# Routed experts on one core: 128-row blocks two groups forward, table-row loads after the transposes

## The reference, cut to what matters

```python
x = x + attention(layernorm(x), Wq, Wk, Wv)
xn = layernorm(x)
shared = (silu(xn @ shared_gate.T) * (xn @ shared_up.T)) @ shared_down.T
probs = sigmoid(xn @ router_w.T + routing_bias)
scores, indices = top_k(probs, 2)          # 2 of 8 experts for each of 4096 tokens
w[t, indices[t]] = scores[t] / sum(scores[t])
g = silu(xn @ gate_w[e]); u = xn @ up_w[e]  # 256 -> 512, e = 0..7
out = x + shared + sum_e w[:, e] * ((g * u) @ down_w[e])
```

## Time and profile before

| | us |
|---|---|
| median of 3 runs (lowest, highest) | 573.29 (572.55, 575.23) |
| the profiled execution | 578.4 |
| its span | 576.6 |
| PE busy | 521.9 (91%) |
| DVE busy | 371.8 (64%) |
| ACT busy | 306.5 (53%) |
| POOL busy | 290.2 (50%) |
| first matmul of the routed part, start | 277.08 |
| last matmul of the program, end | 561.47 |
| last add issued, start | 569.38 |

### The profile page before, as it was taken

How to read it: one execution, slowest core, us unless ns; L and a number is a source line. 1 busy time by engine, 2 the same in 40 slices (tenths; PEclk the granted TensorE clock), 3 DMA queues, 4 the chain that set the end, 5 groups by cost and what they waited for, 6 DMA issues and landing times. The chain is left out here.

```text
span 576.6 us, 14723 instructions
## 1 busy us (share of the span) xinstructions
PE 521.9 (91%) x4521; PEld 422.9 (73%) x4522; DVE 371.8 (64%) x933; ACT 306.5 (53%) x578; POOL 290.2 (50%) x236
## 2 busy tenths in 40 slices
PE   2797999798999999889799999999999999999970
PEld 1455788586777878778578888888888888888860
DVE  5579999879897978969645555455545455545440
ACT  4989778577768667544234443443444443444430
POOL 3654778557585846756014434533433343533443
PEclk9699999899999999989999999999999999999996
DMA  7988866929493948552455646565565555566523
GB/s 260 221 202 149 155 171 132 257 78 217 140 198 125 199 134 170 175 156 76 91 115 88 99 76 94 75 93 74 74 96 81 78 77 75 83 90 77 73 30 36
DMA packets 147551, 70.53 MB, mean 122 GB/s; under 512 B 122384, under 2 KB 140560, under 8 KB 147504
## 3 DMA queue, kind: packets, MB, share of 16 engines
q1 hardware_dynamic: 133904, 50.69, 42.1%
q0 software_dynamic: 13600, 19.22, 19.0%
HBM read 19.48 MB, written 23.54 MB: 75 GB/s over the span
## 5 line engine op out<-in xcount | busy, mean ns | idle before, releaser
L1767 PE MATMUL bank<-xn2t,w 128*128 128x256 f16 x1728 | 197.1, 273 | 2.9 <-DMA xn2t<-rows 2.5
L1767 PEld LDWEIGHTS bank<-xn2t,w 128*128 (+1 forms) x1728 | 168.5, 98 | 26.5 <-issue 2.8
L712 POOL DMA_INDIRECT out<-p,wm x56 | 89.2, 1593 | 115.2 <-DMA out<-p,wm 44.6
L1336 DVE SCALAR_TENSOR_TENSOR th<-th,bank 128x512 f32<-128x512 f32 x88 | 60.1, 683 | 75.3 <-ACT th L806 75.2
L1781 PE MATMUL bank<-w,h 128*128 (+1 forms) x840 | 98.5, 273 | 2.1 <-DVE z L1268 2.0
L1781 PEld LDWEIGHTS bank<-w,h 128*128 128x128 f16 x840 | 81.5, 98 | 13.5 <-DVE z L1268 3.5
L762 ACT ACTIVATE h<-th 128x512 f16<-128x512 f32 x72 | 45.2, 628 | 85.3 <-DVE th L1345 83.5
L806 ACT ACTIVATE th<-bank 128x512 f32<-128x512 f32 x88 | 52.5, 596 | 58.4 <-PE bank L1767 58.2
L1171 DVE TENSOR_TENSOR h<-th,h 128x512 f16<-128x512 f32 x72 | 49.8, 691 | 41.1 <-ACT h L762 41.1
L601 POOL TENSOR_TENSOR w<-wst,w 128x768 f16<-128x768 f32 x36 | 59.1, 1642 | 31.4 <-ACT w L762 31.1
L625 POOL DMA_INDIRECT rows<-xrow,sidx x56 | 57.4, 1026 | 27.5 <-DVE sidx L1328 15.9
(11 more groups left out here) (159 smaller groups left out, 728.3 us busy)
## 6 DMA issues: line engine op xcount, KB each, us to landing
wst<-w_all SPq DMA_DIRECT2D x36, 384.0 KB, 3.6
x<-x SPq DMA_DIRECT2D x8, 512.0 KB, 5.6
out<-x SPq DMA_DIRECT2D x8, 512.0 KB, 4.6
rows<-xrow POOLq DMA_DIRECT2D x1, 1192.5 KB, 7.3
rows<-xrow,sidx POOLq DMA_INDIRECT x56, 4.3
out<-p,wm POOLq DMA_INDIRECT x56, 4.0
wm<-rows SPq DMA_DIRECT2D x28, 9.0 KB, 1.8
xn2t<-rows SPq DMA_TRANSPOSE x28, 3.6
```

The source lines that it names most:

```text
L712: cc.indirect_dma_start(out, bass.IndirectOffsetOnAxis(ap=index, axis=0), part, None, compute_op=ALU.add).then_inc(y_out, 16)
L1336: d.scalar_tensor_tensor(out=tb, in0=tb, scalar=1.0, in1=G[half][:, :], op0=ALU.add, op1=ALU.mult).then_inc(f_sg, 1)
L1767: ins = mm(dst, w_ap(j, ws, m * MAT + k * I + (2 * half + i) * P, P), moving(ms * KD + k), start=(cnt == 0), stop=(cnt == 3 * KD - 1))
```

## The change

Three things are changed, all in the routed part.

1. **The singles run two groups forward.** In group i PE now takes the down product of single i+2 and the gate and up products of single i+3. The first two groups take five gate and up products of singles and four down products, the last group and the one before it take no gate and up product of a single, and the last group no single at all. Each engine follows: order of copies on ACT, of h on DVE, of adds on POOL (p2i-1, s(i+2), p2i), of loads on SP. The last two groups of adds are p23, s14, p24 and then p25, p26, p27.
2. **In SP's queue the transpose of a block stands ahead of its index load,** and the wait on `y_out` moves with the index load.
3. **At the entry** the two table reads of the pairs are made before the wait for the scattered rows, all four row transposes (p0, s0, s1, p1) are issued first, and the four index loads behind them.

```diff
+            def load_pair_rows(row, ring, read):
                 slot = ring % 2
-                row = sp.value_load(start_tab[0:1, ds(n, 1)], min_val=0, max_val=ROWS - TT)
-                gate(sp, ax_in[ring], seen, sp_past)
-                free_aux(used)
-                sp.dma_start(aux[...], rows[ds(row, TT), D:RC]...).then_inc(ax_in[ring], 16)
                 free_rows(read)
                 sp.dma_start_transpose(xt[...], rows[ds(row, TT), 0:D]...).then_inc(xt_in[slot], 16)
+            def load_pair_aux(row, ring, seen, used):
+                gate(sp, ax_in[ring], seen, sp_past)
+                free_aux(used)
+                sp.dma_start(aux[...], rows[ds(row, TT), D:RC]...).then_inc(ax_in[ring], 16)
...
             def first_group():                      # SP
                 hs_transpose(0, 0)
                 row = single_row(2)
                 load_single_rows(row, 0, 1)
                 hs_transpose(1, 1)
                 load_pair(2, 2, 2 * SHARED + 2, 0, 0)
+                load_single_aux(row, 0, 16, 48)
                 hs_transpose(2, 0)
-                load_single_aux(row, 0, 16, 16)
-                load_single(3, 1, 2, 16, 32)
-                load_pair(3, 3, 2 * SHARED + 4, 0, 16)
+                row = single_row(3)
+                load_single_rows(row, 1, 2)
+                load_pair(3, 3, 2 * SHARED + 4, 0, 0)
+                load_single_aux(row, 1, 16, 64)
...
-            def group(i, par, last=False):          # SP
-                load_pair(2 * i + 2, 2 - 2 * par, 4 * i + (2 * SHARED + 2), 8 * i + 8 * par, GROUP_ADDS * i - 16)
-                hs_transpose(i + 2, par)
-                if not last:
-                    load_single(i + 3, 1 - par, i + 2, 8 * i + (16 + 8 * par), GROUP_ADDS * i + 32)
-                load_pair(2 * i + 3, 3 - 2 * par, 4 * i + (2 * SHARED + 4), 8 * i + 8 * par, GROUP_ADDS * i + 16)
+            def group(i, par, single=True):
+                if not isinstance(i, int) or i > 2:
+                    hs_transpose(i + 2, par)
+                if single:
+                    row = single_row(i + 4)
+                    load_single_rows(row, par, i + 3)
+                load_pair(2 * i + 2, 2 - 2 * par, 4 * i + (2 * SHARED + 2), 8 * i + 8 * par, GROUP_ADDS * i)
+                if single:
+                    load_single_aux(row, par, 8 * i + (32 - 8 * par), GROUP_ADDS * i + 48)
+                load_pair(2 * i + 3, 3 - 2 * par, 4 * i + (2 * SHARED + 4), 8 * i + 8 * par, GROUP_ADDS * i + 32)
...
+            def first_groups():                     # POOL
+                y_add(0, 0, 16, 0)
+                y_add_single(0, 0, 16, 32)
+                y_add_single(1, 1, 16, 48)
+                y_add(1, 1, 16, 64)
...
             def first_groups():                     # PE
...
                 pe.wait_ge(xt_in[1], 16)
                 gate_up(t + 1, 0, j1, pair_moving(1), False)
+                down(t, j0)
                 single_down(0, 0)
-                down(t, j0)
                 single_gate_up(2, 0, 32)
+                gate_up(t + 1, 1, j1, pair_moving(1), False)
                 single_down(1, 1)
-                gate_up(t + 1, 1, j1, pair_moving(1), False)
+                j2 = expert(2)
+                pe.wait_ge(xt_in[0], 32)
+                gate_up(t + 2, 0, j2, pair_moving(0), False)
+                down(t + 1, j1)
+                single_gate_up(3, 1, 32)
+                gate_up(t + 2, 1, j2, pair_moving(0), False)
+                single_down(2, 0)
...
```

More of the change, by code:

```diff
@@ L439, in free_aux, with pair_row, single_row @@
                 gate(sp, y_out, used, sp_past)
-            def load_pair(n, ring, read, seen, used):
-                slot = ring % 2
-                row = sp.value_load(start_tab[0:1, ds(n, 1)], min_val=0, max_val=ROWS - TT)
+            def pair_row(n):
+                return sp.value_load(start_tab[0:1, ds(n, 1)], min_val=0, max_val=ROWS - TT)
+            def single_row(k):
+                return sp.value_load(start_tab[0:1, ds(k + PAIRS, 1)], min_val=0, max_val=ROWS - P)
+            def load_pair_rows(row, ring, read):
+                slot = ring % 2
+                free_rows(read)
+                sp.dma_start_transpose(
+                    xt[:, slot * 4 * TT:(slot + 1) * 4 * TT].rearrange("p (c r) -> p c r", r=TT),
+                    rows[ds(row, TT), 0:D].bitcast(F16)).then_inc(xt_in[slot], 16)
+            def load_pair_aux(row, ring, seen, used):
                 gate(sp, ax_in[ring], seen, sp_past)
@@ L449, in load_pair @@
                              ).then_inc(ax_in[ring], 16)
[L450 to L456, removed]
+            def load_pair(n, ring, read, seen, used):
+                row = pair_row(n)
+                load_pair_rows(row, ring, read)
+                load_pair_aux(row, ring, seen, used)
             def load_single_rows(row, slot, read):
@@ L470, in load_single_aux @@
                              rows[ds(row, P), D:RC]).then_inc(as_in[slot], 16)
[L472 to L476, removed]
             def hs_transpose(k, slot):
@@ L517, in _ @@
             first_group()
-            group(1, 1)
-            with sp.Fori(2, GROUPS - 2, 2) as i:
+            second_group()
+            group(2, 0)
+            group(3, 1)
+            with sp.Fori(4, GROUPS - 4, 2) as i:
                 for s in range(2):
                     group(i + s, s)
-            group(GROUPS - 2, 0, last=True)
+            group(GROUPS - 4, 0)
+            group(GROUPS - 3, 1, single=False)
+            group(GROUPS - 2, 0, single=False)
             sp.wait_ge(y_out, 32 * PAIRS + 16 * SINGLES)
@@ L1155, in _ @@
                     group(i + s, s)
-            group(GROUPS - 2, 0)
-            group(GROUPS - 1, 1, last=True)
+            group(GROUPS - 2, 0, single=False)
+            group(GROUPS - 1, 1, single=False, copy_single=False)
             last_copy()
@@ L1712, in ffn, with group @@
                 ffn_low(t, half)
-            def group(i, last=False):
+            def group(i, single=True):
                 t = 2 * i + SHARED
@@ L1717, in group @@
                     ffn(t, half)
-                if not last:
-                    single_h(i + 2)
+                if single:
+                    single_h(i + 3)
                 for half in range(2):
@@ L1730, in _ @@
             ffn(SHARED + 1, 1)
-            with dve.Fori(1, GROUPS - 1) as i:
+            ffn(SHARED + 2, 0)
+            single_h(3)
+            ffn(SHARED + 2, 1)
+            ffn(SHARED + 3, 0)
+            single_h(4)
+            ffn(SHARED + 3, 1)
+            with dve.Fori(2, GROUPS - 2) as i:
                 group(i)
-            group(GROUPS - 1, last=True)
+            group(GROUPS - 2, single=False)
+            group(GROUPS - 1, single=False)
         @block.tensor
@@ L2076, in first_group, with group @@
                 gate_up(t + 1, 0, j1, pair_moving(1), False)
+                down(t, j0)
                 single_down(0, 0)
-                down(t, j0)
                 single_gate_up(2, 0, 32)
+                gate_up(t + 1, 1, j1, pair_moving(1), False)
                 single_down(1, 1)
-                gate_up(t + 1, 1, j1, pair_moving(1), False)
-            def group(i, par, last=False):
+                j2 = expert(2)
[5 more added lines that the diff above has]
+                single_down(2, 0)
+                j3 = expert(3)
+                pe.wait_ge(xt_in[1], 32)
+                gate_up(t + 3, 0, j3, pair_moving(1), False)
+                down(t + 2, j2)
+                single_gate_up(4, 0, 48)
+                gate_up(t + 3, 1, j3, pair_moving(1), False)
+                single_down(3, 1)
+            def group(i, par, single=True, down_single=True):
                 t = 2 * i + SHARED
@@ L2127, in _ @@
                     group(i + s, s)
-            group(GROUPS - 2, 0)
-            group(GROUPS - 1, 1, last=True)
+            group(GROUPS - 2, 0, single=False)
+            group(GROUPS - 1, 1, single=False, down_single=False)
             last_down()
```

107 lines of the change are left out of this document (69 added, 38 removed).

## The result

The changed kernel takes 584.25 us (median of 5 runs, 583.14 to 587.90) against 573.29 for the kernel before (median of 5, 571.86 to 577.74): ratio 1.0168, 95% interval 1.0129 to 1.0207, slower (the two medians alone give 1.0191). A later comparison of the same two on another occasion gave 1.0221 (1.0171 to 1.0271). The forecast was 580.0 in a range of 575 to 585, so the direction and most of the path were right, and one term was far too small. The measured median lies at the upper end of the range; the forecast alone spanned 576 to 582.

The account below looks back on a forecast made before the run. PE's matmuls were taken to bound the routed part, so only PE's idle time and the tail could change. + 7.6 (s3's rows) + 2.5 (clock) + 0.6 (h transposes) - 4.0 (tail) = + 6.7 on 573.29: 580.0 us, range 575 to 585.

Parts of the forecast that it names:

- s3's rows: Entry: s3's row transpose queues behind s2's index load, which waits for adds; PE idles 8.3 us, + 7.6 us, bounds 6.5 to 8.7.
- the reason given for the start of p0's copies: Entry: ACT is held until 292.09 by the landing of s0's h, so p0's copies can't start much before 296.50.
- The clock: s3's block after the long idle gap: PE falls to half clock, + 2.5 us, bounds 0 to 2.5.
- The middle: Middle groups: h transposes issued later, slack 0.8 us with the median landing; + 0.6 us in all, least 0, most 5.
- The rival with the late h transposes: Middle: PE waits for ten h transposes by 0.5 us each, 4.4 more than taken, 584.4 us; chance 0.13.
- named for a right forecast: Gap about 8 us, block at clock 0.50, third add about 305, last matmul about 572, last pair's add about 2 us later.
- the signs named for a wrong one: No gap over 3 us from 300 to 320, many small gaps before singles' downs, or last add over 4 us behind PE.
- The tail: End: last pair's first add 2.1 instead of 6.05 us behind PE's last matmul, - 4.0 us, bounds 3.7 and 4.2.
- The sum: Whole kernel: + 7.6 + 2.5 + 0.6 - 4.0 = + 6.7 us, giving 580.0 us.
- The first case: Entry: PE never waits for s3, entry 0.8 ahead and tail gives 4.0: 568.5 us; chance 0.10.
- the even one: Entry: wait for s3 half as long (4 us) and clock stays up, 573.1 us; chance 0.08.
- the last (the tail gives nothing): Tail: chain of adds falls behind again, p27's add stays 6 us behind PE's last matmul, 584.0 us; chance 0.07.

Follow-up runs that it names:

- second profile: Kernel before and changed kernel each run once more, unchanged: before 574.4 us (one run), changed kernel ratio 1.0221 to before.
- e1: Changed kernel with s3's row transpose moved ahead of s2's index load in SP's queue: 582.0 us, ratio 1.0109 to the kernel before.
- e5: Changed kernel with 28 filler matmuls keeping PE busy while it waits for s3's rows: one run, 312.5 us from S to the end of the span.
- e2: Changed kernel with, in the middle, each single's h transpose moved ahead of the index load that waits for an add: 582.9 us, ratio 1.0106.
- e8: Changed kernel with old entry, row and h transposes first, and each single's index load moved to the next group: 576.8 us, ratio 0.9990.
- e9: Changed kernel, its new entry kept, with row and h transposes first and each single's index load moved to the next group: 573.6 us, ratio 0.9941.
- e3: Changed kernel with s3's rows ahead of s2's index load and, in the middle, h transposes ahead of waiting index loads: 576.5 us, ratio 0.9990.
- e4: Kernel before with only the new order of table reads, transposes and index loads at the entry: 575.9 us, ratio 0.9994.

## Why the prediction was right, and where it was not

**s3's rows: + 7.6 forecast, + 7.9 measured** (44.0 - 36.1; 6.3 in the second profile). The add of s0 was forecast 33.2 us after S (305.0 - 271.79) and came 33.3 after it (302.06 - 268.74). Each link is in the chain shown above, and e1 takes the gap away by putting s2's index load behind the two transposes. That the size fits so well is partly luck. The first profile has the slow blocks at s0, 1.7 us, which push p0's down and with it the whole chain back; in the second, without them, the add of s0 came 32.0 us after S (303.45 - 271.47), and the term is 6.3, just under the lower bound of 6.5. PE's gap was 7.0 us in both, where 8.3 was forecast. And the reason given for the start of p0's copies didn't hold: ACT didn't wait for s0's h in the changed kernel, it copied p0's result from 293.74, 1.3 us after PE had gone on from p0's down (292.47). This down lay so late after S that the copy still came where the forecast had it (25.0 us after S against 24.7).

**The clock: + 2.5 forecast, + 1.9 measured** (4.52 - 2.59), 1.4 in the second profile of the changed kernel, and 2.9 in e2, where the block takes 5.09 us and the one behind it is slow as well. The earlier trace rows was the right row, and e5 shows the cause.

The rule of the Trainium skill (TensorE: Matmul & The Clock Gate, HAM oscillation) holds here as far as it says that a long idle gap brings half clock; the block ran at a granted clock of 0.55.

**The middle: + 0.6 forecast, + 7.3 measured** (262.8 - 1.9 - 253.6). This is the step that failed, by size. The mechanism was the one named, h transposes behind the index load that waits for an add and behind the rows of the next pair, but I priced it with the median landing of before and a slack of 0.8 us. Three things were missing. The slack is that of a chain that runs on time, and in the groups behind the entry it doesn't: s5's h was 2.4 us late and took the clock down again (its next block took 3.87 us for 2.59). Behind such a down the next block comes some 0.6 us late each time, even where the down itself hardly waits, which I put down to the table read between them (argued, as said at e2); in the kernel before this shows at 0.3 us at most. And the landing was slower than the median of before. From issue to landing the transposes of the h of s5 to s14 took 3.1 to 4.2 us in both profiles of before; in the changed kernel they took 5.1, 5.1, 5.4, 3.8, 5.1, 3.7, 3.8, 3.6, 4.3 and 5.0, which uses up most or all of those 4.3 to 5.6 us. The singles whose down or the block behind it came 0.6 us late or more are s5, s6, s7 and s9, four of the five with a landing of 5.0 us or more. No run shows why they are slower. In e2, where h is issued some 12 us ahead, landings of up to 5.8 us cost nothing.

In the first profile the waits at the downs, the reads behind them and the slow block at s5 add up to 6.9 of the 7.3 us, and e2 gives 5.7 back (260.9 to 255.2). The 1.6 us that are left are hardly more than the 1.3 by which the two profiles of before differ. The rival with the late h transposes had this price, 0.5 us for each of ten, and its number, 584.4 us, is nearly the one that was measured (584.25), though the loss isn't spread over ten but sits at four or five of them. It had a chance of 0.13, and that the measured time lies within the range is owed to the room left for it, not to the forecast's own sum. The signs agree: the gap, the slow block, the third add and the short tail came as named for a right forecast, but PE's last matmul ended at 575.5 instead of about 572 although S was 3 us earlier, and one of the signs named for a wrong one, gaps at the singles' downs ended by a DMA into `v`, is there in part (two of them in the first profile).

**The tail: - 4.0 forecast, - 4.5 measured** in the first profiles (6.05 to 1.5), and - 0.9 in the second ones (3.5 to 2.7). All ten profiles in which the singles are forward have p27's add at E + 0.8 to E + 2.7, the three in which they aren't at E + 3.3 to E + 6.1. So the mechanism is right, and its price is nearer to 2 to 3 us than to 4: I had taken a single execution for typical. The steps of the chain came as forecast (p24's to p27's adds at E - 17.9, - 11.2, - 4.8 and + 1.5, against - 18.2, - 11.2, - 4.2 and + 2.1). The 3.3 us that I took for the least from the end of a down to its add isn't a floor in the tail, where p27's add comes 0.8 to 2.7 us behind it; held to it, my own sum would have given E + 3.3.

**The sum** was + 6.7; from S the profiles say 317.4 - 304.8 = + 12.6, and the medians + 11.0. The forecast has the direction and the order of size; the missing 6 us lie in the middle. The first case (faster, PE never waits) and the even one fell with the 7 us gap, and the last (the tail gives nothing) with p27's add at E + 1.5.

Left open: why e8 and e9 differ by 0.5% in their runs, how much of the 2.3 to 3.6 us gained from S in e8 is real, and why the h transposes take longer to land in their new place.

## What to carry to other kernels

In a queue that runs in order a load whose wait depends on the far end of the pipeline must stand behind everything that is needed sooner, however small it is; when work is moved forward, look up every wait of its queue again, with what must now have happened before it. A hidden latency of half a microsecond (here, as argued, a table read) comes out as soon as the wait in front of it is late. And take a price from the place where the change will run: slack that a settled pipeline has in the middle is not there in its first groups, and the landing time of a transfer in its old place (3.1 to 4.2 us here) is not that in its new one (up to 5.4).

## What the runs showed that I had not expected

- The part of the program that no kernel here changes started its last product between 266.6 and 271.8 us (S), and this spread of 5 us is as large as most effects studied. Two profiles can't be compared end to end.
- The clock can fall after shorter gaps too. In the second profile of before, with 0.81 us of idleness, a block of 2.8 us and then 2.30 us of idleness, p0's 24 matmuls took 4.30 us from start to start instead of 2.62, while in the first profile they took their usual time after gaps of 0.85 and 2.50:

```profile
269.06 2.79 PE L1781 MATMUL bank<-w,p 128*128 128x256 f16 x24 [0.81 <-DVE x L1368]
274.15 4.46 PE L1767 MATMUL bank<-xn2t,w 128*128 128x256 f16 x24 [2.30 <-DMA xn2t<-rows]
278.45 2.75 PE L2041 MATMUL bank<-w,ptr 128*128 x12
```

The granted clock of that block is 0.59 (274.2 to 278.4 us). With the new entry the same befell s0's block behind a wait of 2.1 to 2.4 us: it was slow in the first profile of after (granted clock 0.67), in e2, e3 and e4, and took its usual time in the second profile of after, in e1, e5 and e9, behind waits of 2.0 to 2.4. So the length of this gap alone doesn't tell which it will be.
